# The order of the calls on each engine of a two-layer transformer kernel, permuted

## The reference, cut to what matters

```python
x = layernorm(x + attn0(x))    # q, k of width 16, causal softmax(q k^T / 4) @ x
x = layernorm(x + ffn0(x))     # one 256x256 weight, quantized to {-s, 0, s}
x = layernorm(x + attn1(x))    # per-token similarity of q and k, one step of a small
                               # convolution network over the tokens, softmax over tokens,
                               # times v, times a channel gate, projection
x = layernorm(x + moe(x))      # h = layernorm(x)*gamma + beta; shared expert (512 wide, silu)
                               # + the top one of 8 such experts, scaled by its probability
```

## Time and profile before

| | us |
|---|---|
| median of 3 executions | 792.61 |
| lowest and highest | 790.55, 793.23 |
| span of the profiled execution | 794.0 |
| TensorE busy in it | 721.3 (91%) |
| VectorE busy | 699.8 (88%) |
| ScalarE busy | 656.5 (83%) |
| GpSimd busy | 335.0 (42%) |

### The profile page before, as it was taken

One profiled execution on the slowest core, in us unless ns is written; L12 is line 12 of the kernel. 1 busy time (PEld: TensorE's weight loads), 2 busy tenths in 40 slices (PEclk: granted clock), 3 DMA queues, 4 the chain that ended last, 5 costly groups with the idle time before them and its releaser, 6 DMA issues.

```text
span 794.0 us, 18530 instructions
## 1 busy us (share of the span) xinstructions
PE 721.3 (91%) x5417; PEld 546.5 (69%) x5417; DVE 699.8 (88%) x2124; ACT 656.5 (83%) x1447; POOL 335.0 (42%) x370
## 2 busy tenths in 40 slices
PE   3769998999999999999999999999989977988882
PEld 2556686777767767776776777777777766777771
DVE  5767888899989999998999999999899988998885
ACT  2265759997997998799799789988899976999994
POOL 3000011124334343342523335354567775876667
PEclk9979999999999999999999999999999998999996
DMA  8104301123132131213223023021624447455430
GB/s 264 35 15 119 106 2 55 34 90 98 55 107 70 55 129 43 80 61 108 87 61 114 29 80 108 14 88 41 211 71 149 145 152 206 147 177 163 136 119 30
DMA packets 57217, 76.51 MB, mean 96 GB/s; under 512 B 15453, under 2 KB 37919, under 8 KB 57120
## 3 DMA queue, kind: packets, MB, share of 16 engines
q1 hardware_dynamic: 46016, 48.45, 21.5%
q0 software_dynamic: 9600, 25.25, 8.9%
q10 hardware_dynamic: 1504, 1.64, 0.6%
HBM read 47.42 MB, written 28.91 MB: 96 GB/s over the span
## 4 chain that ended last, share of the span: by engine, by line
PE 67%; DVE 9%; ACT 8%; issue 7%; POOL 3%; DMA 3%; SPq 1%; ACTq 1%; DVEq 0%; POOLq 0%
PE bank L677 9%; PE bank L902 6%; PE bank L889 5%; PE bank L758 4%; PE bank L770 4%; PE bank L626 3%; PE bank L760 3%; PE bank L759 3%; ACT G_S L1845 3%; PE bank L1112 2%; POOL out L4113 2%; PE bank L705 2%; PE bank L716 2%; PE bank L706 2%; PE bank L855 2%
## 5 line engine op out<-in xcount | busy, mean ns | idle before, releaser
L4008 POOL TENSOR_TENSOR R<-rstd,mhalf 128x4 f32<-128x4 f32 x16 | 19.2, 1199 | 261.8 <-DVE rstd L2268 261.8
L4113 POOL DMA_INDIRECT out<-G_y,Gid x72 | 81.7, 1135 | 45.6 <-ACT G_y L1866 24.6
L1845 ACT ACTIVATE G_S<-bank,e1b,e1s 128x256 f32<-128x256 f32 (+1 forms) x188 | 87.1, 580 | 5.9 <-PE bank L1095 5.8
L1112 PE MATMUL bank<-E2T,split 128*128 x576 | 74.6, 284 | 14.5 <-DVE split L3053 11.9
L677 PE MATMUL bank<-X,PT 128*128 128x257 f32 x320 | 83.5, 401 | 0.5 <-ACT PT L1574 0.4
L1095 PE MATMUL bank<-G_T,E1T 128*128 128x256 f16 (+1 forms) x752 | 75.6, 251 | 7.8 <-issue 6.4
L4052 POOL DMA_INDIRECT rrec<-R,pos x64 | 67.8, 1060 | 30.7 <-issue 22.5
L1112 PEld LDWEIGHTS bank<-E2T,split 128*128 128x128 f16 x576 | 56.5, 101 | 27.4 <-issue 18.4
L4043 POOL DMA_INDIRECT hrec<-HN,pos x64 | 67.1, 1049 | 16.7 <-issue 15.9
L1095 PEld LDWEIGHTS bank<-G_T,E1T 128*128 x752 | 60.5, 99 | 17.9 <-issue 10.7
L677 PEld LDWEIGHTS bank<-X,PT 128*128 128x128 f32 x320 | 60.1, 200 | 10.5 <-issue 1.4
(11 more groups left out here) (438 smaller groups left out, 2292.8 us busy)
## 6 DMA issues: line engine op xcount, KB each, us to landing
XT<-in_xT SPq DMA_DIRECT2D x16, 512.0 KB, 4.0
X<-in_x SPq DMA_DIRECT2D x16, 512.0 KB, 6.0
G_h<-hrec SPq DMA_DIRECT2D x25, 257.0 KB, 3.5
G_r<-rrec SPq DMA_DIRECT2D x25, 257.0 KB, 3.4
e1n<-in_ew SPq DMA_DIRECT2D x8, 512.0 KB
e2n<-in_ew SPq DMA_DIRECT2D x8, 512.0 KB, 3.5
G_h<-hrec SPq DMA_DIRECT2D x22, 128.5 KB, 2.4
G_r<-rrec SPq DMA_DIRECT2D x22, 128.5 KB, 2.5
```

The source lines that it names most:

```text
L1112: last = pe.matmul(down_bank(w)[:, j * D:(j + 1) * D], x[w % NGB][:, f, j * P:(j + 1) * P], E2T[:, expert_of[w, j], f, :], start=k == 0, s ...
L1845: last = act.activation(G_S[w % NGS][:, ff, a:b], bk[:, o + a:o + b], ACT.Silu, bias=e1b[:, e, ff], scale=e1s[:, e, ff])
L4113: pool.indirect_dma_start(t["out"], bass.IndirectOffsetOnAxis(Gid[w % NGI][:, j:j + 1], 0), G_y[w % NGY][:, j, :], None, bounds_check=TOK ...
```

## The change

It gives each engine's calls in another order, SyncE's among them. The calls, their waits and their number stay. Cut to what the prediction speaks of:

```diff
 # SyncE
         sp.dma_start(wqk[:], first[0][1]).then_inc(s["wqk"], 16)
 
+        load_e2(0)
+        load_x(0)
+        load_e1(0)
         load_xT(0)
-        load_e1(0)
-        load_x(0)
-        load_e2(0)
-        load_xT(1)
+        load_tiny()
         load_small()
         load_x(1)
+        load_xT(1)
+        load_x(2)
         load_e1(1)
-        load_tiny()
         load_e2(1)
-        load_x(2)
         load_xT(2)
+        one_e1(0)
+        load_xT(3)
         pad_rows()
-        load_xT(3)
-        one_e1(0)
...
+        maxima(15)
         load_x(15)
-        maxima(15)
 # TensorE, start
         scoreT(0, 0)
+        m_sum()
         scoreT(0, 1)
-        m_sum()
+        rest_gate()
+        scoreT(0, 2)
+        pv(0, 0)
+        scoreT(0, 3)
+        pv(0, 1)
         map_et0(0)
-        scoreT(0, 2)
-        scoreT(0, 3)
-        for i in range(3):
-            pv(0, i)
-        rest_gate()
+        pv(0, 2)
         pv(0, 3)
         proj(1)
         x1T(0, 0)
         score(1, 0)
+        x1T(0, 1)
+        score(1, 1)
         map_dg(0)
-        score(1, 1)
+        score(1, 2)
         map_et1(0)
-        x1T(0, 1)
         ffn(0, 0)
-        score(1, 2)
         score(1, 3)
 # TensorE, a part of the steady loop
             x1T(2 * g, 1)
+            dqk(2 * g - 1, 2)
             up(2 * g - 3, 0)
-            dqk(2 * g - 1, 2)
             dqk(2 * g - 1, 3)
+            score(2 * g + 1, 0)
+            score(2 * g + 1, 1)
             rank(2 * g - 3)
-            score(2 * g + 1, 0)
             ffn(2 * g, 0)
-            score(2 * g + 1, 1)
             up(2 * g - 3, 1)
 # TensorE, late
+        gdown(11, 0)
         gTr(14)
+        gdown(11, 1)
         gup(13, 0)
-        gdown(11, 0)
-        gdown(11, 1)
         gup(13, 1)
         gTr(15)
+        gup(14, 0)
+        gdown(12, 0)
+        gup(14, 1)
+        gdown(12, 1)
         gTr(16)
-        gdown(12, 0)
-        gdown(12, 1)
-        gup(14, 0)
+        gup(15, 0)
         gTr(17)
-        gup(14, 1)
-        gup(15, 0)
 # VectorE, start
+        map0(0, 0)
         scale(0)
+        map0(0, 1)
         rest(0)
-        map0(0, 0)
+        map1(0, 0)
+        scale(1)
         rest(1)
-        scale(1)
-        map0(0, 1)
-        map1(0, 0)
+        qklo(0)
         scale(2)
         rest(2)
-        qklo(0)
 # VectorE, late: before
-        gnb_(7)
-        gy(9)
-        gve(8)
-        gTl(12)
-        mix(2)
-        gx(9)
-        mix(3)
...
-        mix(8)
-        gve(10)
-        gy(11)
-        mix(9)
-        gTl(14)
-        gSl(12)
 # VectorE, late: after
+        gy(9)
+        gTl(12)
+        mix(4)
...
+        gx(9)
+        gmv(8, 1)
+        mix(5)
+        gve(8)
+        gbn(9, 0)
+        gnb_(7)
...
+        gTl(14)
         gmv(10, 0)
+        gmv(10, 1)
+        gSl(12)
+        gve(10)
         mix(7)
-        gmv(10, 1)
+        gy(11)
         mix(8)
 # VectorE, tail loop
             gbn(w - 7, 1)
+            gy(w - 6)
             gmv(w - 7, 0)
-            gTl(w - 2)
             gmv(w - 7, 1)
             gve(w - 7)
             gSl(w - 5)
-            gy(w - 6)
             gnb_(w - 7)
             gx(w - 6)
+            gTl(w - 2)
 # GpSimd
-        hsc(11, 3)
         rsc(10, 3)
-        hid(13)
         power1(15)
         power2(13)
+        hsc(11, 3)
...
-        gid_(11)
         gpower(6)
-        gid_(12)
-        scatter(5, 0)
-        rsc(15, 0)
         scatter(5, 1)
-        rsc(15, 1)
-        rsc(15, 2)
         scatter(6, 0)
         gpower(7)
         scatter(6, 1)
         gpower(8)
         scatter(7, 0)
+        scatter(7, 1)
+        gpower(9)
+        rsc(15, 0)
+        scatter(8, 0)
+        gid_(11)
+        scatter(8, 1)
+        rsc(15, 1)
+        gid_(12)
+        rsc(15, 2)
+        gpower(10)
+        rsc(15, 3)
         gid_(13)
-        scatter(7, 1)
-        rsc(15, 3)
-        gpower(9)
-        scatter(8, 0)
-        scatter(8, 1)
-        gpower(10)
         scatter(9, 0)
```

More of the change, by code:

```diff
@@ L1120, in pe_program @@
         w_all()
[L1121 to L1122 removed]
+        score(0, 0)
+        score(0, 1)
+        score(0, 2)
         w0T()
@@ L1182, in pe_program @@
         u(0, 0)
-        for i in range(3):
-            pv(2, i)
+        pv(2, 0)
+        pv(2, 1)
         u(0, 1)
+        pv(2, 2)
         x2T(1, 0)
@@ L1940, in act_program @@
         exp(3, 0)
-        for i in range(3):
-            x2s(2, i)
+        x2s(2, 0)
+        x2s(2, 1)
         exp(3, 1)
+        x2s(2, 2)
         exp(3, 2)
@@ L3786, in dve_program @@
         ode(7, 26)
-        rg(13)
-        for i in range(4):
-            x3(14, i)
+        x3(14, 0)
+        x3(14, 1)
+        x3(14, 2)
+        x3(14, 3)
         y(13, 0)
+        y(13, 1)
         x3(15, 0)
-        y(13, 1)
         ve2(14)
+        x3(15, 1)
+        x3(15, 2)
+        x3(15, 3)
+        gTl(3)
         y(13, 2)
+        gy(0)
         y(13, 3)
+        gSl(1)
         r(13, 0)
         r(13, 1)
-        x3(15, 1)
-        gTl(3)
-        x3(15, 2)
-        x3(15, 3)
-        gy(0)
-        gSl(1)
+        gx(0)
         HTl_(14, 0)
@@ L3862, in dve_program @@
         gbn(3, 0)
-        place(15, 1)
+        gbn(3, 1)
         sort(2)
-        place(15, 2)
-        router(15, 7)
-        gTl(7)
-        sort(3)
-        gbn(3, 1)
-        Sl_(14, 0)
-        Sl_(14, 1)
-        gmv(3, 0)
-        gy(4)
-        gnb_(2)
-        gmv(3, 1)
-        gx(4)
-        gve(3)
-        rg(15)
-        sort(4)
+        gmv(3, 0)
+        Sl_(14, 0)
+        sort(3)
+        Sl_(14, 1)
+        gmv(3, 1)
+        gy(4)
+        sort(4)
+        gnb_(2)
+        gTl(7)
@@ L3880, in dve_program @@
+        gx(4)
+        router(15, 7)
+        sort(5)
         Sl_(14, 2)
         Sl_(14, 3)
+        sort(6)
+        gTl(8)
         gbn(4, 0)
         gbn(4, 1)
-        gTl(8)
+        gve(3)
+        sort(7)
+        y(14, 0)
+        y(14, 1)
+        gSl(5)
+        y(14, 2)
+        y(14, 3)
         gmv(4, 0)
         gmv(4, 1)
-        sort(5)
-        gve(4)
-        gSl(5)
-        y(14, 0)
-        gnb_(3)
-        for i in range(1, 4):
-            y(14, i)
-        gnb_(4)
-        r(14, 0)
@@ L3911, in dve_program @@
-        Sl_(15, 3)
-        gmv(5, 0)
+        sort(10)
+        rg(15)
+        gx(6)
+        mix(0)
         gmv(5, 1)
-        gx(6)
+        gbn(6, 0)
         gve(5)
-        gbn(6, 0)
+        mix(1)
+        gSl(7)
         gbn(6, 1)
-        gSl(7)
-        gmv(6, 0)
-        y(15, 0)
-        y(15, 1)
-        gmv(6, 1)
-        gnb_(5)
-        y(15, 2)
+        y(15, 0)
+        gnb_(5)
+        y(15, 1)
+        mix(2)
+        y(15, 2)
+        mix(3)
+        gmv(6, 0)
         y(15, 3)
-        gve(6)
@@ L3927, in dve_program @@
[L3927 removed]
         gSl(8)
         gy(7)
[L3930 to L3943 removed]
+        gmv(6, 1)
+        gx(7)
+        gTl(10)
+        gbn(7, 0)
+        r(15, 0)
+        gbn(7, 1)
+        gSl(9)
+        gve(6)
+        gy(8)
+        gmv(7, 0)
+        gTl(11)
+        gmv(7, 1)
@@ L4222, in pool_program @@
         rsc(14, 2)
+        scatter(4, 1)
+        scatter(5, 0)
         rsc(14, 3)
-        gpower(5)
-        scatter(4, 1)
-        gid_(11)
+        gid_(10)
+        hsc(15, 3)
         gpower(6)
-        gid_(12)
-        scatter(5, 0)
-        rsc(15, 0)
         scatter(5, 1)
-        rsc(15, 1)
-        rsc(15, 2)
         scatter(6, 0)
```

1246 lines of the change are left out of this document (647 added, 599 removed).

## The result

The changed kernel takes **815.02 us** (median of 4, 813.89 to 816.59), the kernel before, beside it, 791.58 (788.57 to 793.23). The ratio is 1.0289, 95% interval 1.0258 to 1.0321: 23.4 us slower. The forecast was 792.0, its range ended at 799.0, and the worst rival gave 797. The profiled execution took 816.59 us with a span of 815.3, against 794.0 before, so the two traces differ by 21.3 us.

The account below looks back on a forecast made before the run. TensorE was taken as the bound from 60 to 640 us, with gains only at the start and 640 to 680. Terms +3.5 + 0 + 0 - 4 + 0 = -0.5 gave 792.1, stated as 792.0 us; range 786.5 to 799.

Parts of the forecast that it names:

- Part 1: First 60 us: XT loaded fourth delays the first projection by 6.1 us, partly regained; +3.5 us at 60 us.
- Rival 4: Start: XT pays nothing for its place because landings don't follow issue order; 786.7 us, chance 0.11.
- Part 2: Steady loops, 140 to 560 us: lists permuted inside a step change nothing; 0, ends -0.5 and +5 us.
- Rival 5: Steady loops: a moved call finds its operand late in each step, +5 us; 797 us, chance 0.08.
- Part 3: Load x(15) moved behind maxima(15): starts 5 us later but stays hidden by 1.3 us; 0.
- Part 4: Tail, 640 to 680 us: reordering removes much of two TensorE waits; -4 us, ends -6.7 and +1.5.
- the two links: Tail: gpower(7) behind rsc(15) calls, gy(9) behind gnb_(7); cutting both removes the first hole whole, 3.3 us.
- The 8.6 us: Tail, 640 to 680 us: price of two TensorE waits, 2.07 and 3.68, plus slower gdown matmuls behind them.
- Rival 2: Tail: late gid_ calls delay gload(16) to (18), the hole only moves, about +0.7 us; 796.8 us, chance 0.29.
- deciding point: Tail: gload(16) issued after 659.6 us, plus 3.5 for the late start, makes the second hole longer than before.
- Part 5: Tail loop from 680 us: ScalarE is full and its work unchanged; 0, or +2 us if gnb_ costs.
- The +2 for gnb_: Tail loop: moved gnb_ might cost 0.1 us in each of some twenty steps, +2 us.

Follow-up runs that it names:

- e18: Repeat of e1 beside e17 on one chip: kernel before with changed start and steady loops, tail as before; 798.92 us, ratio 1.0099.
- e17: Kernel before with only the steady loops' calls in the changed order on all engines, start and tail as before; 795.63 us, ratio 1.0054.
- e4: Kernel before with only the load of XT(0) moved from first to fourth of SyncE's large loads; 798.1 us, ratio 1.0063.
- e5b: Kernel before with only rsc(15,0..3) behind gpower(9), gy(9) ahead of gnb_(7), and gTl(14) ahead of gmv(10,0) and gve(10); ratio 1.0027.
- e6b: Kernel before with only GpSimd's gid_(9) to gid_(13) moved later as in the changed kernel; ratio 1.0011.
- e9: e2 with gpower(4) moved directly behind gpower(3) and gpower(6) directly behind scatter(4,1), ahead of other scatters; 816.71 us, ratio 1.0099 to the kernel before.
- e8b: Kernel before with only VectorE's gmv(6,1), gve(6) and gnb_(6) moved behind gy(7), gx(7) and gbn(8,0); ratio 1.0003.
- e1: Kernel before with all engines' start and steady loops in the changed order, remaining calls as before; 799.31 us, ratio 1.0087.
- e16: Kernel before with larger buffer rings: six G_y, twelve Gid, six pairs of gathered-row buffers; 810.41 us, ratio 0.9998.
- e13: The changed kernel itself, timed again on a slower chip against the kernel before; 843.84 us, ratio 1.0402.
- e7b: Kernel before with only GpSimd's scatters of h of batches 14 and 15 moved behind the first output scatters, gid_(9) behind gpower(4); ratio 1.0025.
- e10: Changed kernel with TensorE's calls behind its steady loop in the order of before; ratio 1.0468 to the kernel before.
- e12: Changed kernel with the load of XT(0) first again among SyncE's large loads; 840.7 us, ratio 1.0384 to the kernel before.
- e15: Changed kernel with six G_y, twelve Gid and six pairs of gathered-row buffers, order unchanged; 834.24 us, ratio 1.0269 to the kernel before.
- e2: Kernel before with only GpSimd's calls behind its steady loop in the changed order; 807.59 us, ratio 1.0192.

## Why the prediction was wrong

**Part 1, the start: right.** +3.5 was forecast, 3.6 measured (e18 less e17), though so close an agreement is partly luck: the difference is uncertain by about 2 us. The steps hold too: projection 14.2 forecast and 14.50 read, score(0,0) 23.2 and 23.30, the gate's wait gone, proj(1) 43.4 and 43.09. XT's place alone costs +5.0 (e4), inside the ends of 1.5 and 6.1. That the tiny loads give back the rest fits, but wasn't tried by itself. "TensorE is full until 640" was read too widely: the earlier trace rows leave out 100 to 140 and 560 to 600, where the kernel before has it busy 37.23 and 37.39 us of 40. Rival 4 falls. Order of issue, not some other order, set the landings: the first large load took 4.2 us before (the median of XT's two) and 5.0 after, the fourth 11.3 and 11.7, though the tiles had changed places.

The Trainium skill (DMA: Bandwidth & Descriptors, Queues, rings and completion order) says that a later transfer may finish its writes before an earlier one. Taken alone it left room for XT to pay nothing. The trace doesn't contradict it as a warning about correctness, but for time the landings in order of issue decide.

**Part 2, the steady loops: a term mis-sized.** 0 was forecast, with +5 as the end; +4.3 measured (e17). Rival 5 named the mechanism, a moved call that finds its operand late in every step, and had the price (0.8 a step), but 0.08 of the chance. The reason I gave for 0, that TensorE has only 1.42 us of idle time, was a reason against a gain and none against a loss. In a stretch where an engine is 99.7% busy, a permutation can't win and can lose.

**Part 3, x(15): right.** No wait for it shows, and projection 15 and what follows it move with the rest.

**Part 4, the hole: the step that failed.** -4 was forecast, and the tail gave +15 to +16 (1.0289 of the changed kernel against 1.0099 and 1.0087 of its head). Three things in that step were wrong.

1. I counted the two links that the change cuts and took the next wait on the same chain to be late by one or two microseconds. But cutting them gave nothing even by itself: in e5b (1.0027) both waits are gone from the trace and other waits, of 3.33, 2.27 and 2.52 us, stand in their place. The 8.6 us were read off waits as if each could be taken away alone.
2. I followed the delay of gid_(11) from the calls in front of it at their durations of before, and got 657 us for gload(16). It was issued at 673.55. The calls in front of it had waits of their own in the new order, 3.07 and 2.86 us for ScalarE's G_y, and 2.9 for gid_(9) earlier on. The estimate took durations and left waits out, and it left out that all of the region would be late by then (gTr(13) by 12.0 us).
3. The rows that the step was built on began at 640. The losses begin at 600, where VectorE and ScalarE were full and I had nothing to say but "full": +3.6 at gTr(0), +10.6 at gTr(9), +12.0 at gTr(13). A stretch in which two engines are full and all lists are permuted has little cover: VectorE had 0.58 us idle of 40 there, ScalarE 0.68.

Rival 2 had the sign and a part of the mechanism: gload(16) after its deciding point, G_h late, the hole moved. It priced the tail at +0.7, a single hole traded for another. And the late gid_ that it named costs nothing that shows when it is moved alone (e6b). The region holds many such trades, and each wait moves the operands of the next.

**Part 5, the tail loop: wrong in its premise.** "ScalarE is full there, and its work is the same": it is busy 50.15 us of 60 and no longer full. The prediction had named this, and TensorE waiting between 60 and 560, as signs that it was wrong altogether; both came. The +2 for gnb_ has its rows (it waits 21 times where it had waited once), but how much of that reaches the end isn't told apart from the rest of the tail.

**What stays open.** That the tail's 16 us are a matter of lists that don't fit is borne out by every exchange tried, but not shown for the whole: GpSimd's or ScalarE's changed list put alone into the kernel before costs 1.9 or 2.6%, GpSimd's or TensorE's old one put into the changed kernel gives nothing back, moving two powers ahead leaves 1.0% of GpSimd's loss (e9), and single late calls cost nothing that shows (e6b to e8b). Reuse of buffers is 9.6 us of 31.3 on the chip where it was tried. VectorE's tail list wasn't exchanged, and which of the moves carry the rest hasn't been told apart.

## What to carry to other kernels

In a hand-ordered kernel on several in-order engines, a wait that goes away is worth only what the next wait behind it allows. Read that one first, and give a permuted stretch with full engines a price above zero. Cost a moved call by what stands ahead of it in the new list including those calls' own waits, and check the pairs that cross engines (a power and its reader, a copy of indices and the load that waits for it) before single calls. Exchanging the list of one engine is a poor test of that engine's order: it tests the fit.

## What I had not expected of the hardware

**The chip.** The kernel before took 791.58, 792.48 and 791.92 us beside the changed kernel, e1 to e4, and e17 and e18, and 812.4, 809.18 and 812.55 on the three other chips, 2.2 to 2.6% more, with nothing in between. The changed kernel took 815.02 us in the first group and 843.84 in the second, so its own ratio went from 1.0289 (1.0258 to 1.0321) to 1.0402 (1.0351 to 1.0453). The mean granted clock doesn't account for it: 0.977 in the changed kernel's profile of the first group, 0.965 in that of the second, and 0.978 for e16 on the slower chip, 0.975 for the kernel before on the faster. The traces of the second group have waits that end by something the trace only calls remote, and none of the eight of the first has one. Waits of VectorE in e13:

```profile
DVE r_lg L2452 <- remote: 23.3, 6, 4.3
```

In one of them TensorE's matmuls of the logits start at 226.50 and take 0.55 us, and VectorE reads them at 231.10, after an idle time of 4.19 us. In e13 such waits are up to 4.3 us long, in e7b one of VectorE's lasts 11.5. Durations of instructions and landings of transfers are alike in both groups. What these waits are stays open.

They do show where the changed kernel loses more on these chips. The waits at r_lg, 21 to 24 us in all, stand in the five traces of the second group that have the changed loops (e10, e12 to e15) and in none that has the loops of before. At projection 15, ahead of the whole tail, those five stand 19.2 to 21.6 us behind the trace of before, the other seven of the group 5.6 to 12.4. In the first group the four with the changed start and loops stand 4.2 to 5.8 us behind it, and e2, which has both of before, 1.8 us ahead. The medians of the changed and the old are 9.2 us apart in the second group and 5.6 in the first, so some 4 us more are lost up to there, an estimate from these shifts. Comparisons of small differences belong on one chip.

**A wait for an output buffer can go without a gain that shows.** 5.8 us of VectorE's waits for output scatters went with two more buffers, and the time moved by 0.25%, with 1.0351 to 1.0453 and 1.0327 to 1.0427 as the two intervals: a small gain isn't excluded. A wait that is large in the table isn't on the path for that reason alone.
